# Adjacency build of a four-layer GNN kernel: banks opened by one column, counts stored in four pieces

## The reference

```python
edge_index = jnp.stack([src, dst])
h = jnp.maximum(_layernorm(x, axis=-1), 0.0)
x = x + _L0_gnn_ref(h, edge_index, ...)      # segment_sum(x[src], dst) @ W_rel + b_rel + x @ W_root, batch norm, relu
h = jnp.maximum(_layernorm(x, axis=-1), 0.0)
x = x + _L1_gnn_ref(h, ..., src, dst)        # two mean aggregations (divided by the in-degree)
h = jnp.maximum(_layernorm(x, axis=-1), 0.0)
x = x + _L2_gnn_ref(h, edge_index, ...)      # attention over edges, 8 heads, softmax by destination
h = jnp.maximum(_layernorm(x, axis=-1), 0.0)
x = x + _L3_gnn_ref(h, ..., edge_index, edge_type_8)   # two relational layers, 8 edge types
```

## Time and profile before

| | us |
|---|---|
| median of 3 runs | 3777.47 |
| range of the runs | 3775.76 to 3778.92 |
| the profiled execution | 3770.99 |
| its span, first to last instruction | 3769.6 |
| first register load to last epoch's copy (the build) | about 65 to 485 |
| busy in the span: TensorE, VectorE, ScalarE, GpSimd | 3028.6, 2390.8, 1261.2, 1989.3 |
| products that open banks (L648), 336 of 500 columns | 111.0 |

### The profile page before, as it was taken

The page is one execution under the profiler, slowest core; times in us unless marked ns, Lnnn a source line. Parts: engine busy times, 40 slices in busy tenths (PEclk is TensorE's granted clock), DMA queues, the critical chain, the costliest instruction groups (busy, mean ns, idle before and its releaser), DMA issues. The chain is left out here.

```text
span 3769.6 us, 52194 instructions
## 1 busy us (share of the span) xinstructions
PE 3028.6 (80%) x16694; PEld 2344.0 (62%) x16694; DVE 2390.8 (63%) x3938; ACT 1261.2 (33%) x2681; POOL 1989.3 (53%) x2077
## 2 busy tenths in 40 slices
PE   5666689899688888888886479999888878787886
PEld 3555544455466666666664248888787577777775
DVE  7777768446698888888888656665555333333333
ACT  2334401100134344444433358777775200000000
POOL 4000000000277777777773157777777477777776
PEclk8788789899899999999998679999999989899987
DMA  3444475447344544444541145555555655555553
GB/s 133 182 200 210 189 322 229 187 185 291 91 114 114 116 117 114 110 117 116 117 110 43 67 149 217 202 216 195 194 201 190 233 194 195 195 195 194 195 194 93
DMA packets 236209, 633.91 MB, mean 168 GB/s; under 512 B 59204, under 2 KB 179506, under 8 KB 221088
## 3 DMA queue, kind: packets, MB, share of 16 engines
q1 hardware_dynamic: 170632, 494.18, 35.4%
q0 software_dynamic: 65312, 136.39, 14.0%
HBM read 412.69 MB, written 217.68 MB: 167 GB/s over the span
## 5 line engine op out<-in xcount | busy, mean ns | idle before, releaser
L1752 POOL DMA_INDIRECT edge_buffers<-rel_table,relidx x1222 | 1155.7, 946 | 459.4 <-issue 284.6
L1069 POOL DMA_INDIRECT round_buffers<-xs_t,srcs x806 | 766.2, 951 | 569.9 <-DMA xd_t<-round_buffers 324.5
L1795 PE MATMUL sums<-count_windows,H 128*128 128x208 f32 x3800 | 855.7, 362 | 30.6 <-ACT trio L1941 28.8
L1869 DVE TENSOR_TENSOR trio<-trio,sums 128x128 f32 x1242 | 356.9, 287 | 685.7 <-PE sums L1767 492.4
L1795 PEld LDWEIGHTS sums<-count_windows,H 128*128 128x128 f32 x3800 | 684.0, 203 | 47.3 <-issue 29.4
L1767 PE MATMUL sums<-edge_buffers 128*128 128x128 f32 x2340 | 372.4, 293 | 162.1 <-DMA edge_buffers<-rel_table,relidx 155.0
L1767 PEld LDWEIGHTS sums<-edge_buffers 128*128 128x128 f32 x2340 | 340.0, 202 | 190.1 <-DMA edge_buffers<-rel_table,relidx 156.1
L889 POOL IOTA trio<- 128x806 int32 x1 | 0.8, 806 | 604.0 <-ACT H L538 604.0
L1213 ACT ACTIVATE trio<-sums 128x128 f32 x806 | 223.8, 278 | 278.9 <-PE sums L1191 204.9
L1113 PE MATMUL sums<-round_buffers,ident 128*128 128x408 f32 x620 | 279.2, 534 | 30.6 <-DMA round_buffers<-xs_t,srcs 29.2
L1116 PEld LDWEIGHTS sums<-round_buffers 128*128 128x128 f32 x1612 | 243.5, 198 | 76.5 <-issue 66.1
(11 more groups left out here) (361 smaller groups left out, 4531.9 us busy)
## 6 DMA issues: line engine op xcount, KB each, us to landing
step_counts<-count_windows SPq DMA_DIRECT2D x38, 2600.0 KB, 9.2
count_windows<-step_counts SPq DMA_DIRECT2D x38, 2600.0 KB, 10.0
chunk_and_window<-adj SPq DMA_DIRECT2D x10, 5600.0 KB, 16.1
round_buffers<-xd_t SPq DMA_DIRECT2D x806, 68.0 KB
adj_chunk<-adj SPq DMA_DIRECT2D x9, 5600.0 KB, 16.6
adj<-adj_window SPq DMA_DIRECT2D x11, 3850.0 KB, 11.5
adj<-chunk_and_window SPq DMA_DIRECT2D x10, 3850.0 KB, 10.9
rel_table<-table_stages SPq DMA_DIRECT2D x50, 512.0 KB, 2.6
```

The source lines that it names most:

```text
L1069: nc.gpsimd.indirect_dma_start(rows[r % RING][:, k * RW:(k + 1) * RW], None, xs_t[:, :], bass.IndirectOffsetOnAxis(ap=srcs[:, t:t + 1], ax ...
L1752: nc.gpsimd.indirect_dma_start(slot(p * IG + i, k), None, rel_t[p][:, :], bass.IndirectOffsetOnAxis(ap=relidx[:, i * U + k:i * U + k + 1], ...
L1795: m = nc.tensor.matmul(pb[4][:, 0:SW * R].rearrange("p (s r) -> p s r", r=R), H[:, h, :], counts[:, w % 2, :, h * R:(h + 1) * R], start=(h ...
L1869: nc.vector.tensor_tensor(held, held, part_of(g)[:, j * P:(j + 1) * P], ALU.add).then_inc(added_n, 1)
```

## The change

It does four things.

- Opening: the banks are opened by a product of one column (column 511, which no step uses) in place of 500; only the first two epochs open all 512 columns. The closing product goes to the same column 511. So a column on which no step adds is no longer zero but keeps what an earlier epoch left.
- Carry: because of that, an epoch whose first block is not the last block of the epoch before takes its carried counts from a block of zeros behind the window (`SPANNED * CELLS`), for which the window buffers are one block longer; three more operations on `steprow` work this out.
- Stores: a window is stored by four DMAs of 32 partitions each, so `s_adj` counts 64 for a window. Except for the last two windows, piece g waits until TensorE has opened the banks of epoch g of the next window (new mark `eload_n`, set by the last of the four opening products).
- Waits: TensorE now waits for the memsets of the two window buffers.

```diff
-        stepped = V.did(V.after().tensor_tensor(carry[:, 1:WINDOWS, 0], b0w[:, 1:WINDOWS, 0], b0w[:, 0:WINDOWS - 1, 0],
-                                                ALU.subtract))
+        V.did(V.after().tensor_tensor(carry[:, 1:WINDOWS, 0], b0w[:, 1:WINDOWS, 0], b0w[:, 0:WINDOWS - 1, 0], ALU.subtract))
+        V.did(V.after().tensor_tensor(b0[:, 1:EPOCHS], bs0[:, 1:EPOCHS, 0], bs0[:, 0:EPOCHS - 1, STEPS_OF - 1], ALU.is_equal))
+        begun = steprow[0:1, 1:EPOCHS, STEPS_OF]
+        V.did(V.after().scalar_tensor_tensor(out=begun, in0=begun, scalar=float(SPANNED * CELLS), in1=b0[:, 1:EPOCHS],
+                                             op0=ALU.subtract, op1=ALU.mult))
+        stepped = V.did(V.after().tensor_scalar(begun, begun, float(SPANNED * CELLS), None, ALU.add))
...
-        filled = [tmp(build, "adj_window", [P, SPANNED * CELLS]), arena[:, 0:SPANNED * CELLS]]
+        filled = [tmp(build, "adj_window", [P, (SPANNED + 1) * CELLS]), arena[:, 0:(SPANNED + 1) * CELLS]]
...
                 for j in range(4):
-                    nc.tensor.matmul(half[:, j * 512:j * 512 + SLOTS // 4 * CELLS], zeros[:, 0:P],
-                                     zeros[:, 0:SLOTS // 4 * CELLS], start=True, stop=False)
+                    first = 0 if e < 2 else 511
+                    m = nc.tensor.matmul(half[:, j * 512 + first:(j + 1) * 512], zeros[:, 0:P], zeros[:, first:512],
+                                         start=True, stop=False)
+                m.then_inc(eload_n, 1)
...
+                if e == 1:
+                    nc.tensor.wait_ge(*wiped[0])
+                if e == GROUP + 1:
+                    nc.tensor.wait_ge(*wiped[1])
...
                 for j in range(4):
-                    m = nc.tensor.matmul(half[:, j * 512:j * 512 + 1], zeros[:, 0:P], zeros[:, 0:1], start=False, stop=True)
+                    m = nc.tensor.matmul(half[:, j * 512 + 511:j * 512 + 512], zeros[:, 0:P], zeros[:, 0:1],
+                                         start=False, stop=True)
...
-                    nc.scalar.wait_ge(s_adj, 16 * (w - 1))
+                    nc.scalar.wait_ge(s_adj, 16 * PIECES_OF * (w - 1))
...
                 if w:
-                    nc.sync.wait_ge(s_adj, 16 * w)
-                nc.sync.dma_start(adj[:, bass.ds(first, SPANNED * CELLS)], filled[w % 2][:, :]).then_inc(s_adj, 16)
+                    nc.sync.wait_ge(s_adj, 16 * PIECES_OF * w)
+                n = P // PIECES_OF
+                for g in range(PIECES_OF):
+                    if w < WINDOWS - 2:
+                        nc.sync.wait_ge(eload_n, GROUP * (w + 1) + g + 1)
+                    nc.sync.dma_start(adj[g * n:(g + 1) * n, bass.ds(first, SPANNED * CELLS)],
+                                      filled[w % 2][g * n:(g + 1) * n, 0:SPANNED * CELLS]).then_inc(s_adj, 16)
```

More of the change, by code:

```diff
@@ L70 @@
 GROUP = 4
+PIECES_OF = 4
 WINDOWS = EPOCHS // GROUP
@@ L608, in build @@
         s_adj = sem("s_adj_stored")
-        root_n = sem("s_first_root")
+        root_n, eload_n = sem("s_first_root"), sem("s_epoch_loaded")
         s_held = [Dma(sem("s_chunk0")), Dma(sem("s_chunk1"))]
@@ L640, in count_edges @@
                 place = nc.values_load_multi_w_load_instructions(
-                    steprow[0:1, e, 0:SLOTS], engines=(ENG.PE,), min_val=0, max_val=(SPANNED - 1) * CELLS,
+                    steprow[0:1, e, 0:SLOTS], engines=(ENG.PE,), min_val=0, max_val=SPANNED * CELLS,
                     skip_runtime_bounds_check_because="made on the chip from counts")[1]
@@ L726, in build @@
         dsum = B1T[:, NP - DST:NP].rearrange("p (b w) -> p b w", w=WD)
-        nc.sync.wait_ge(s_adj, 16 * WINDOWS)
+        nc.sync.wait_ge(s_adj, 16 * PIECES_OF * WINDOWS)
         nc.sync.wait_ge(eout_n, EPOCHS)
```

## The result

The changed kernel takes 3900.61 us (median of four runs, 3898.09 to 3901.81), the kernel before beside it 3778.18 us (3775.76 to 3778.92): 1.0324 times as long, 95% interval 1.0306 to 1.0342, or 122.4 us more. The profiled execution took 3901.81 us. I had predicted 3804.5 us and a range that ended at 3880. The direction was right, and the size was four and a half times too small.

The account below looks back on a forecast made before the run. TensorE's instruction stream was taken to bound the build; +9.5 us for the windows and +17.6 for the tail made +27 on 3771.0, 3798 us profiled, 3804.5 as median with 6.5 added; 8-in-10 range 3735 to 3880 us.

Parts of the forecast that it names:

- What bounds the stage: Adjacency build: TensorE's own instruction stream sets the pace, 20.0 us a window, with register loads slowed by stores.
- Opening with one column: Bank openings in the build: bounds 0 and 0.4 us gained an epoch, 0.15 taken, 12 us over 82 epochs.
- Bookkeeping: Three more VectorE operations of about 0.2 us and the wait for wiped buffers, in the build: cost nothing.
- Pieces of 4.5 us: Window stores: each 32-partition piece travels 4.5 us, between bounds of 2.5 and 5.1 us.
- The DMA share of the build: A sign in the build's profile: DMA share rises from 0.47 at 198 GB/s to about 0.9 at the same GB/s.
- The store chain as a second bound near 20 us: The SP queue's stores in the build: four pieces in a chain take 19.8 us a window, spending 9 us of slack.
- I take it that only pieces of the half in which partition 0 lies (pieces 0 and 1) slow it: Register loads in the build: only pieces 0 and 1 lengthen them, by 3 and 2 us a window.
- the chain of TensorE: Build windows: 15.4 us plus load losses makes 20.4 us; with the stores 20.5 taken against 20.0, +9.5 us over 19.
- rival C: Register loads in the build: every piece slows them, whatever its partitions; +97 us with the tail, 3875 us; chance 0.18.
- A: The prediction's main case for the build and its tail: 3804.5 us, own range 3782 to 3841; chance 0.40.
- The tail: Last two windows, stored unpaced in series with the aggregation's loads: 18 us each instead of 9.2, +17.6 us.
- The 6.5 us between profile and median: Whole kernel: the earlier runs' median lies 6.5 us above the profiled time, added to 3798 us.

Follow-up runs that it names:

- e1: The changed kernel with each window stored whole by one DMA, without the wait for TensorE; one-column openings and bookkeeping stay: 1.0014 times the kernel before.
- e2: The kernel before with only the four stores of 32 partitions, paced by the last 500-column opening product of an epoch: 1.0379 times the kernel before.
- b1: The changed kernel with four column pieces over 128 partitions, each released by an epoch's closings instead of its openings: 0.9906 times the kernel before.
- b2: The kernel before, openings wide and its own bookkeeping, with four column pieces over 128 partitions released by the closings: 0.9877 times the kernel before.
- e3: The changed kernel with the four pieces cut by columns (128 partitions x 1925 columns) instead of by partitions, same pacing: 0.9958 times the kernel before.
- e4: The changed kernel without the waits on `eload_n`, its four pieces of 32 partitions issued back to back: 1.0246 times the kernel before.
- b3: The changed kernel with its pieces of 32 partitions released by an epoch's closings instead of its openings: 1.0248 times the kernel before.
- b4: The kernel before with column pieces released by the closings, same kernel as b2, on another chip: 3707.44 us against 3772.79, ratio 0.9826.

## Why the prediction was wrong

- **What bounds the stage: right.** TensorE's stream, above all its register load, still does.
- **Opening with one column: taken at 0.15 us an epoch, measured 0** (e1: rest of an epoch 2.64 against 2.63; e2, wide at the same low clock: 2.63; b1 against b2: 2.66 and 2.64). With narrow openings the steps simply spread: 2.4 to 2.8 us for the 19 instead of the 1.8 of the earlier trace rows. The term's lower bound held, its 12 us did not exist. That instruction issue sets the 2.64 us is the reading that fits; no run changed the number of instructions.
- **Bookkeeping: right.** The first register load starts at 64.4 us and at 64.8 before. TensorE's wait for the wiped buffers is an added one (ScalarE keeps its own), not a moved one, and no idle time of TensorE is put down to it.
- **Pieces of 4.5 us: right,** 4.8 us. The Trainium skill ("SBUF — State Buffer", "Door 1: The DMA port swizzle") gives an estimate of 4.5 us by 8 of 16 ports (about 218 GB/s), and e3, the same bytes from 128 partitions, landing in 3.7 instead of 6.1 us, agrees. The DMA share of the build rose to 0.74 at 154 GB/s and not to 0.9 at 198, because TensorE gave the pace and not the stores.
- **The store chain as a second bound near 20 us: not the bound.** SP waited 391 us for TensorE's marks and 63 us for its stores, and ScalarE never waited for a store. TensorE was far slower than I had it.
- **"I take it that only pieces of the half in which partition 0 lies (pieces 0 and 1) slow it": this is the step that failed.** Beside pieces 0, 1, 2 and 3 the loads are 4.1, 3.8, 3.7 and 3.5 us in the mean. Pieces 0 and 1 cost 5.1 us a window, and I had counted 5; pieces 2 and 3 cost another 4.5 us, and I had put them at nothing. Together that is 15.05 - 4 x 1.36 = 9.6 us of loss in each window. With the missing gain of the openings (0.6 a window) the chain of TensorE is 4 x 4.0 + 9.6 = 25.6 us instead of 20.5, and 105 us up to the start of window 20 instead of 9.5. It is rival C's mechanism, and its sign (all loads are long) is the one seen, with 2.4 us lost per load where C had 2.2, and 0.15 us more in an epoch. The halves do differ, but only in size: 6.2 to 6.3 us against 5.2 to 5.3 for a load wholly in the traffic (e4, b3). I gave C 0.18 although its reason against, the chunk load, speaks of writes to SBUF and says nothing of which partitions are read; no row separated the halves, so A and C deserved equal weight, and the range should have held C's own spread. The range ended 5 us above C's middle, and the result lies 26 above it.
- **The tail: 17.6 us taken, 15.6 measured.** The four loads of window 20 are 16.5 us against 9.8 in the kernel before, and the window ends 7.1 us further behind than it began; from ScalarE's last copy to the second chunk are 43.8 us against 35.3, 8.5 more. The size was near, the picture was not: I had both stores in series with the aggregation. Only the last is; the one before it travels beside the last window's epochs and lengthens their loads. TensorE idled 8.10 us ahead of the first chunk, not 16.
- **The low clock** was not in the sum. It fell to 0.50 in the build with the narrow openings, and e1 prices it together with the openings: 0 to 0.28% of the whole, nothing in the epochs.
- **The sum as measured:** 105 us up to window 20 and 15.6 for the tail, 120.6 us at the second chunk, against 122.4 in the medians. The 6.5 us between profile and median that I carried over were -1.2 us after.

## What to carry to other kernels

A register load on TensorE's queue is work on the critical path like any other, and a DMA that reads SBUF beside it makes it up to three to five times as long: cut such a store over all 128 partitions and release it by a mark that lets it fall between two loads, as b4 does, which gave 1.7% with eleven new lines. Pacing is worth something only if the piece is shorter than the gap that it is meant for. And where two outcomes differ by a property that no row of the trace separates, give both the same chance and let the range hold the dearer one.

## What the runs showed of the hardware

- The register load of 20 numbers from one partition takes 1.36 us in quiet, 1.36 to 1.38 beside HBM-to-HBM copies or loads into SBUF, 3.36 beside the store of another tile (325 GB/s), 4.35 in the traffic of a store of 128 partitions (395 GB/s), and 6.2 to 6.3 (partitions 0 to 63) or 5.2 to 5.3 (64 to 127) in that of stores of 32 partitions, though these move half as many bytes a second (493 KB in 2.39 us, 206 GB/s). The numbers lay in partition 0 each time, so whether the half that holds them is what matters is open. The Trainium skill ("SBUF — State Buffer", "SBUF: two separate sides") says that engine ports and DMA ports cannot contend; this load, 4.35 us beside a store against 1.36 in quiet, does not fit that, and the measurement decides.
- 16 packets of 30.8 KB from 32 partitions take 2.39 us each, from 128 partitions 1.16 us.
- An epoch's 2.64 us outside the load were the same within 0.03 us in runs with granted clocks of 0.50 and 0.92, and with openings of 500 columns and of one. In e1 the granted clock was 0.50 (1.2 GHz) over the whole build, and the time was at most 0.28% longer.
